# Four graph layers on one core: where the squares of adj are turned, and where the bias pieces of the attention are made

## The chip, the cores and the metric

The kernel runs on one core of one Trainium2 chip. The metric is the device time of one execution in microseconds, less is better. Before the change the median of 3 runs was 3029.25 us (3028.38 to 3029.67).

## The reference

x is 4096 x 256 and adj is 4096 x 4096, both float32. adj is symmetric in where it is nonzero, not in its values; some 0.8% of it is nonzero. Four layers follow one another, each wrapped in a residual sum and a LayerNorm over the 256 columns:

```
x = layernorm(x + attention(x, adj))       # layer 0: 4 heads of 64, scores + graph_bias * adj,
                                           #   -1e9 where adj == 0, softmax over the keys, @ Wout + bout
x = layernorm(x + gat(x, adj))             # layer 1: leaky_relu(src_i + dst_j), masked by adj > 0,
                                           #   softmax over j, @ (x @ W)
x = layernorm(x + gcn(x, adj))             # layer 2: D^-1/2 adj D^-1/2 @ x @ W.T + b
x = layernorm(x + relu(gcn(x, adj) @ W))   # layer 3
```

Layers 2 and 3 need adj with its rows on the free axis. The kernel makes a turned copy of adj, `adjT`, in the chip's memory beforehand and reads it back in those two layers.

## The kernel before, in words

One program per engine, written out by hand: what stands earlier in an engine's program runs earlier, and semaphores order the engines against one another. SP issues nearly all transfers, in program order; GpSimd (POOL) and ScalarE (ACT) issue a few.

**Layer 0, attention** (`layer0_attention`). 16 chunks of 256 query rows. A chunk goes over 4 heads, each in two halves: 8 sides, each of four beats r = 0 to 3, so that a place in the chunk is written (side, r). In a beat TensorE makes the scores of one piece of 128 x 1024 (L583; these belong to a head 12 beats ahead), turns exponentiated probabilities (L596), and at the end of the side multiplies them with the values (L609). VectorE reads each score piece out of PSUM, adding the bias and taking the maximum (`read_scores`, L869); ScalarE takes exponentials (L720) and copies turned pieces (L729). Three PSUM places of 128 x 1024 are used in turn, so TensorE can't write the third score piece of a side (r = 2) before VectorE has read the second (r = 1), nor turn its second piece of probabilities before VectorE has read r = 0.

The bias of the next chunk is 8 pieces of 128 x 1024 (i = 0 to 7). SP loads them at the 12th to the 19th beat. Six of them ("narrow") are masked by GpSimd in halves of 512 (L506), through three mask buffers, and VectorE finishes each with two operations of 128 x 512 (`make_bias`, L820). The other two (`WIDE`) are done by VectorE alone, in two operations of 128 x 1024 (`make_wide_bias`, L831 and L833). `MAKE_BIAS` says in which beat, after the score read, each piece is made; the first score piece that needs piece i is read at the beat i of side 5 on, (5, 0) for i = 0 up to (6, 3) for i = 7.

adjT is made here, in 256 blocks of 512 rows x 128 columns: SP loads a block (L397), VectorE turns its squares of 32 x 32 in one operation (`turn_block`, L889), SP stores it with four transfers of 64 KB (L408). Two buffers are used in turn, so VectorE waits before a block until the one two before has been stored. `BLOCKS_AT` gives the 17 beats of a chunk that turn a block each; the blocks last for 15 chunks and one more.

**Layer 1, graph attention** (the first half of `graph_layers`). 8 chunks c of 512 rows, each of 16 pairs. In a pair TensorE turns weights (L1462, `turn_pair`) and multiplies (L1479); ScalarE copies the turned weights out (L1604, `keep_pT`), then sums one item of 128 x 1024 of the next chunk's adj in place (L1586, `add_rows`), then takes one exponential (L1596); VectorE and GpSimd mask items (L1175), VectorE takes maxima (L1723) and logits (L1771). SP loads the next chunks' adj in four quarters of 1024 columns, 2 MB each, into `weight` (`load_adj`, L1255), two buffers of four quarters. Quarter n of chunk c + 2 is loaded once TensorE has turned 4(n + 1) pairs of chunk c. ScalarE comes to the items of quarter 3 of chunk c + 1 at pair 8 of chunk c. In VectorE's program `add_out` (L1788 and statistics) follows pair 4 and `ln.normalise` (L135) pair 7.

**Layers 2 and 3.** 8 chunks each. SP loads adjT (L1265), ScalarE and VectorE split it into a high and a low part (L1629, L1817), TensorE multiplies three times (L1532 to L1534).

## Time and profile before

| | before |
|---|---|
| median of 3 runs | 3029.25 us |
| profiled execution | 3032.35 us, of which its span is 3030.6 us |
| TensorE busy | 2951.2 us, 97% |
| VectorE busy | 2098.9 us, 69% |
| ScalarE busy | 1885.9 us, 62% |
| GpSimd busy | 769.0 us, 25% |
| attention, to about | 1615 us |
| layer 1, to about | 2205 us |
| layers 2 and 3, to the end | 3030.6 us |

The span is the time between the first and the last instruction of the profiled execution; 1.75 us of its own time lie around it. In rows of instructions the first number is the start, the second how long the group took; "idle before <- releaser" is how long the engine stood still and whose work ended that.

### The profile page before, as it was taken

To read this page: it belongs to the slowest core of one execution; us is meant where nothing else is said; L and a number is where in the kernel's file an instruction comes from. 1 tells how busy PE (TensorE), PEld (TensorE's weight loads), DVE (VectorE), ACT (ScalarE), POOL (GpSimd) and SP (SyncE) were. 2 spreads that over 40 slices of the span, in tenths; PEclk is the share of its full clock that TensorE was granted. 3 is DMA by queue.
4 is the path that set the end of the run, shared out by engine and by line. 5 is a ranking of instruction groups with operands and counts; after the bars stand their busy time and mean duration, and the time that the engine had idled before them with its cause. 6 is when DMAs were issued, how large, how long until landed. Compare 5 with 4: busy or idle time off the path is not lost.

```text
span 3030.6 us, 45417 instructions
## 1 busy us (share of the span) xinstructions
PE 2951.2 (97%) x16612; PEld 2181.2 (72%) x16612; DVE 2098.9 (69%) x3607; ACT 1885.9 (62%) x2705; POOL 769.0 (25%) x454
## 2 busy tenths in 40 slices
PE   8999999999999999999998899999999999999998
PEld 5777777777777777777776555555558888788886
DVE  6777777777777877787757977777535555565454
ACT  3677777777777777777775677777653333433332
POOL 2123321233212332133301455545501101000000
PEclk9999999999999999999999999999999999999999
DMA  6556676566755667566636333433179988989882
GB/s 186 158 170 198 198 211 180 170 197 196 216 162 180 199 188 227 156 184 205 189 101 257 124 125 130 148 126 125 32 183 214 214 200 201 221 209 217 199 200 58
DMA packets 412525, 534.42 MB, mean 176 GB/s; under 512 B 39440, under 2 KB 341776, under 8 KB 395920
## 3 DMA queue, kind: packets, MB, share of 16 engines
q1 hardware_dynamic: 387264, 445.00, 52.8%
q10 hardware_dynamic: 18144, 66.07, 7.1%
q0 software_dynamic: 6896, 20.45, 2.3%
q8 instruction: 133, 2.18, 0.3%
q14 instruction: 88, 0.72, 0.1%
HBM read 443.29 MB, written 88.08 MB: 175 GB/s over the span
## 4 chain that ended last, share of the span: by engine, by line
PE 80%; DVE 9%; issue 5%; DMA 3%; ACT 2%; POOL 1%; SPq 1%; DVEq 0%; POOLq 0%; ACTq 0%
PE at_o L609 12%; PE gl_four L1479 12%; PE at_turn L583 9%; PE at_turn L596 7%; PE gl_quad L1532 7%; PE gl_quad L1533 7%; PE gl_quad L1534 7%; PE at_score L583 4%; PE at_score L596 4%; PE gl_quad L1462 3%; DVE at_probs L869 2%; DVE at_bias L820 2%; PE gl_four L1505 2%; PE at_mixed L618 2%; DMA adjT<-at_probs 1%
## 5 line engine op out<-in xcount | busy, mean ns | idle before, releaser
L720 ACT ACTIVATE at_probs<-at_probs,at_minus_max 128x1024 f32<-128x1024 f32 x512 | 581.6, 1139 | 9.7 <-DVE at_minus_max L874 8.8
L869 DVE CUSTOM_DVE_ANT_0 at_probs<-at_turn,at_bias 128x1024 f32<-128x1024 f32 x336 | 407.3, 1212 | 170.2 <-PE at_turn L583 164.0
L506 POOL TENSOR_SCALAR at_masked<-at_bias 128x512 bf16<-128x512 f32 x180 | 378.2, 2116 | 537.7 <-DMA at_bias<-in_adj 405.4
L729 ACT ACTIVATE at_pT<-at_turn 128x1024 f32<-128x1024 f32 x342 | 346.0, 1024 | 235.4 <-PE at_turn L596 235.3
L609 PE MATMUL at_o<-at_pT,at_values 128*64 128x256 f32 x4096 | 470.3, 382 | 0.0
L1479 PE MATMUL gl_four<-gl_early,gl_first_wh 128*128 128x512 f32 x1024 | 462.3, 594 | 4.6 <-ACT gl_early L1604 4.6
L1629 ACT ACTIVATE gl_split<-gl_units 128x1024 fp32r<-128x1024 f32 x256 | 263.8, 1055 | 278.6 <-PE gl_quad L1534 278.6
L1532 PE MATMUL gl_quad<-gl_split,gl_rows_hi 128*128 128x512 f32 x1024 | 402.3, 393 | 5.0 <-DVE gl_split L1817 5.0
L609 PEld LDWEIGHTS at_o<-at_pT,at_values 128*64 128x64 f32 x4096 | 282.4, 137 | 172.8 <-issue 43.2
L583 PE MATMUL at_turn<-at_kT,at_q 128*128 128x512 f32 x1344 | 396.0, 416 | 10.3 <-DVE at_maxima L869 10.3
L1533 PE MATMUL gl_quad<-gl_split,gl_rows_hi 128*128 128x512 f32 x1024 | 398.5, 389 | 0.0
L1534 PE MATMUL gl_quad<-gl_split,gl_rows_lo 128*128 128x512 f32 x1024 | 398.5, 389 | 0.0
L1817 DVE TENSOR_TENSOR gl_split<-gl_units,gl_split 128x1024 fp32r<-128x1024 f32 x256 | 306.2, 1222 | 116.2 <-ACT gl_split L1629 115.7
L596 PE MATMUL at_turn<-all_ident,at_probs 128*128 128x128 f32 x2736 | 349.3, 273 | 5.3 <-DVE at_maxima L869 2.9
L596 PEld LDWEIGHTS at_turn<-all_ident,at_probs 128*128 128x128 f32 x2736 | 313.8, 140 | 44.7 <-DVE at_maxima L869 9.0
L1479 PEld LDWEIGHTS gl_four<-gl_early,gl_first_wh 128*128 128x128 f32 x1024 | 185.3, 191 | 190.3 <-issue 185.0
L1175 POOL TENSOR_SCALAR gl_first_weights<-gl_first_weights 128x1024 f32<-128x1024 f32 x57 | 237.4, 4165 | 268.1 <-ACT gl_first_weights L1586 268.1
L583 PEld LDWEIGHTS at_turn<-at_kT,at_q 128*128 128x128 f32 x1344 | 227.8, 189 | 73.9 <-issue 30.6
L869 DVE CUSTOM_DVE_ANT_0 at_probs<-at_score,at_bias 128x1024 f32<-128x1024 f32 x176 | 213.4, 1212 | 93.3 <-PE at_score L583 90.4
L729 ACT ACTIVATE at_pT<-at_score 128x1024 f32<-128x1024 f32 x170 | 174.1, 1024 | 114.0 <-PE at_score L596 113.9
L889 DVE STREAM_TRANSPOSE at_probs<-at_probs 128x512 f32<-128x512 f32 x256 | 181.2, 708 | 84.1 <-DMA adjT<-at_probs 83.5
L1604 ACT ACTIVATE gl_early<-gl_quad 128x1024 f32<-128x1024 f32 x128 | 131.0, 1023 | 157.2 <-PE gl_quad L1462 157.2
(135 smaller groups left out, 3871.0 us busy)
## 6 DMA issues: line engine op xcount, KB each, us to landing
gl_units<-adjT SPq DMA_DIRECT2D x512, 256.0 KB, 7.8
at_bias<-in_adj SPq DMA_DIRECT2D x128, 512.0 KB, 6.5
at_probs<-in_adj SPq DMA_DIRECT2D x256, 256.0 KB, 3.7
adjT<-at_probs SPq DMA_DIRECT2D x1024, 64.0 KB, 3.0
gl_first_weights<-in_adj SPq DMA_DIRECT2D x32, 2048.0 KB, 8.2
at_values<-v_heads ACTq DMA_DIRECT2D x126, 512.0 KB, 4.4
gl_early<-x SPq DMA_DIRECT2D x160, 128.0 KB, 2.6
x<-gl_early POOLq DMA_DIRECT2D x64, 128.0 KB, 2.8
```

Source lines behind the costliest of these rows:

```text
L506: pool.tensor_scalar(masked[:, g % MASKS, :], part, 0.0, MASKED / SCALE, ALU.is_equal, ALU.mult)\
L583: last = pe.matmul(place[:, at], q[:, q_place(h), part, t * P:(t + 1) * P], kT[:, h, col:col + BANK], start=part == 0, stop=part == 1)
L596: last = pe.transpose(place[:, a * CN + t * P:a * CN + (t + 1) * P], ring[:, place_in_ring(s, m // BEATS), t, m % BEATS * P:(m % BEATS + 1 ...
L609: last = pe.matmul(o_bank[side * HD:(side + 1) * HD, 0:CN], values[:, q, a, :], pT[:, slot, a % GROUP * CN:(a % GROUP + 1) * CN], start=q ...
L720: act.activation(part, part, ACT.Exp, bias=minus_max[:, k, t:t + 1], scale=1.0, accum_out=sums[:, k, t, pp:pp + 1]).then_inc(prob_ready, 1)
L729: act.activation(pT[:, j % PT_SLOTS, :], place[:], ACT.Copy).then_inc(pT_ready, 1)
L869: dve.tensor_tensor_reduce(out=ring[:, place_in_ring(u, pp), t, :], in0=place[:], in1=bias[:, t, at], scale=SCALE, scalar=LOWEST, op0=ALU. ...
L1479: last = pe.matmul(out_bank1[c % 2][half], wh[:, m * D + half * P:m * D + (half + 1) * P], pT[:, g % PT_RING, part * CN:(part + 1) * CN], ...
L1532: pe.matmul(out_bank3[r % 2][half], rows_hi[:, at], block_hi, start=first, stop=False)
L1533: pe.matmul(out_bank3[r % 2][half], rows_hi[:, at], block_lo, start=False, stop=False)
L1534: last = pe.matmul(out_bank3[r % 2][half], rows_lo[:, at], block_hi, start=False, stop=final)
L1817: dve.tensor_tensor(split3[:, slot, 1, :], tiles[:, n, part:part + 2 * CN], split3[:, slot, 0, :].bitcast(F32), ALU.subtract).then_inc(lo3 ...
```

## The change

Eight of the 32 blocks of 128 columns of each of six sets of 512 rows (sets 2 to 7, columns 3072 to 4095: 48 of 256 blocks) are no longer turned in the attention. They are turned in layer 1, the second layer, out of quarter 3 of the adj chunk that lies in `weight` for that layer anyway, so they aren't loaded for it. VectorE turns two blocks each after pairs 3, 5, 6 and 7 of chunks 1 to 6, through two buffers; SP stores each with four transfers, in its program between the loads of quarters 0 and 1 of chunk c + 2; ScalarE doesn't go on at pair 8, which overwrites that quarter in place, before all eight have been turned. The attention has 208 blocks left, and three of the 17 beats of a chunk, (4, 2), (5, 0) and (6, 3), turn none.

The bias pieces are made at other beats: 1 and 2 together at (4, 3), 3 at (5, 1), 4 and 5 together at (5, 3), 6 at (6, 1), 7 at (6, 2), and none at (5, 2) and (6, 0). The two wide pieces are 2 and 5 in place of 3 and 6.

```diff
-    MAKE_BIAS = {(4, 1): 0, (4, 3): 1, (5, 1): 2, (5, 2): 3, (5, 3): 4, (6, 0): 5, (6, 1): 6, (6, 2): 7}
+    MAKE_BIAS = {(4, 1): (0,), (4, 3): (1, 2), (5, 1): (3,), (5, 3): (4, 5), (6, 1): (6,), (6, 2): (7,)}
...
-    ROW_BLOCKS = N // P
-    BLOCKS = NT // BLOCK_TILES * ROW_BLOCKS
+    LATE_BLOCKS = 8
+    SET_BLOCKS = N // P
+    ROW_BLOCKS = SET_BLOCKS - LATE_BLOCKS
+    WHOLE_SETS = 2
+    BLOCKS = WHOLE_SETS * LATE_BLOCKS + NT // BLOCK_TILES * ROW_BLOCKS
...
-    BLOCKS_AT = {(0, 0): 1, (0, 2): 1, (1, 0): 1, (1, 2): 1, (2, 1): 1, (2, 2): 1, (2, 3): 1, (3, 0): 1, (3, 1): 1, (3, 2): 1, (4, 0): 1, (4, 2): 1, (5, 0): 1, (6, 3): 1, (7, 0): 1, (7, 1): 1, (7, 2): 1}
+    BLOCKS_AT = {(0, 0): 1, (0, 2): 1, (1, 0): 1, (1, 2): 1, (2, 1): 1, (2, 2): 1, (2, 3): 1, (3, 0): 1, (3, 1): 1, (3, 2): 1, (4, 0): 1, (7, 0): 1, (7, 1): 1, (7, 2): 1}
...
-    WIDE = (3, 6)
+    WIDE = (2, 5)
...
-                        if (side, r) in MAKE_BIAS and not last:
-                            i = MAKE_BIAS[side, r]
+                        for i in () if last else MAKE_BIAS.get((side, r), ()):
...
+    LATE_AT = {3: (0, 1), 5: (2, 3), 6: (4, 5), 7: (6, 7)}
...
+        turned_squares = early[:, 4096:4096 + 2 * CN].rearrange("p (b k t i) -> p b k t i", b=2, k=BLOCK_KEYS, t=CT)
...
+            def store_late(c, k):
+
+                b = LATE_BLOCKS * (c + 1 - WHOLE_SETS) + k
+                n = N // P - LATE_BLOCKS + k
+                sync.wait_ge(late_turned, b + 1)
...
+                for g in range(SQUARES):
+                    rows = slice(g * CT * SQUARE, (g + 1) * CT * SQUARE)
+                    sync.dma_start(to[:, (c + 1) * (N // CN) + n * P // CN, at:at + BLOCK_KEYS, rows],
+                                   turned_squares[g * SQUARE:(g + 1) * SQUARE, b % 2, :, :, :].rearrange("j k t i -> j k (t i)"))\
+                        .then_inc(late_stored[b % 2], 16)
...
+                    if n == 0 and c + 1 >= WHOLE_SETS:
+                        for k in range(LATE_BLOCKS):
+                            store_late(c, k)
+            for stored_late in late_stored:
+                sync.wait_ge(stored_late, 16 * SQUARES * LATE_BLOCKS * (CHUNKS - WHOLE_SETS) // 2)
...
+                if c >= WHOLE_SETS and n == QUARTERS - 1 and t == 0:
+                    act.wait_ge(late_turned, LATE_BLOCKS * (c + 1 - WHOLE_SETS))
...
+            def turn_late(c, k):
+
+                b = LATE_BLOCKS * (c + 1 - WHOLE_SETS) + k
+                n = QUARTERS - 1
+                dve.wait_ge(adj_loaded[(c + 1) % 2 * QUARTERS + n], 16 * ((c + 1) // 2 + 1))
+                wait(dve, late_stored[b % 2], 16 * SQUARES * (b // 2))
+                block = weight[:, (c + 1) % 2, n, :, k * P:(k + 1) * P]
+                dve.transpose(turned_squares[:, b % 2, :, :, :], block.rearrange("p t (k i) -> p k t i", i=SQUARE))\
+                   .then_inc(late_turned, 1)
...
                     logits(e - 3)
+                    if WHOLE_SETS <= c + 1 < CHUNKS:
+                        for k in LATE_AT.get(pair, ()):
+                            turn_late(c, k)
                     if pair == 4 and c:
                         add_out(c - 1)
```

## Rows read from the trace of the kernel before

**Rows 1.** The page: busy time of each engine

```profile
PE 2951.2 (97%) x16612; PEld 2181.2 (72%) x16612; DVE 2098.9 (69%) x3607; ACT 1885.9 (62%) x2705; POOL 769.0 (25%) x454
```

**Rows 2.** Windows, a chunk each of attention and layer 1: length, PE, PEld, DVE, ACT, POOL, PEclk

```profile
480.30:575.70 95.40, 94.42 (x672) 73.14 (x671) 73.84 (x141) 71.76 (x106) 26.70 (x14) 1.00 0.63 192
...
1882.00:1953.00 71.00, 70.03 (x265) 38.09 (x264) 54.28 (x83) 51.50 (x81) 37.09 (x15) 1.00 0.36 133
```

**Rows 3.** TensorE in order of time, attention: its idle times, four of them

```profile
173.11 1.19 PE L583 MATMUL at_score<-at_kT,at_q 128*128 128x512 f32 x4 [0.98 <-DVE at_maxima L869]
...
553.60 1.19 PE L583 MATMUL at_turn<-at_kT,at_q 128*128 128x512 f32 x4 [0.98 <-DVE at_maxima L869]
...
817.85 1.20 PE L583 MATMUL at_score<-at_kT,at_q 128*128 128x512 f32 x4 [2.49 <-DVE at_maxima L869]
...
1508.99 1.19 PE L583 MATMUL at_turn<-at_kT,at_q 128*128 128x512 f32 x4 [0.98 <-DVE at_maxima L869]
```

**Rows 4.** VectorE in order of time, sides 5 and 6 of the same chunk

```profile
538.14 1.23 DVE L869 CUSTOM_DVE_ANT_0 at_probs<-at_score,at_bias 128x1024 f32<-128x1024 f32 x1 [1.90 <-PE at_score L583]
...
544.04 1.05 DVE L831 TENSOR_SCALAR at_xs<-at_bias 128x1024 bf16<-128x1024 f32 x1
545.13 1.51 DVE L833 SCALAR_TENSOR_TENSOR at_bias<-at_bias,at_gain,at_xs 128x1024 f32<-128x1024 f32 x1
546.67 1.23 DVE L869 CUSTOM_DVE_ANT_0 at_probs<-at_turn,at_bias 128x1024 f32<-128x1024 f32 x1
...
547.82 1.41 DVE L820 SCALAR_TENSOR_TENSOR at_bias<-at_bias,at_gain,at_masked 128x512 f32<-128x512 f32 x2
549.36 1.23 DVE L869 CUSTOM_DVE_ANT_0 at_probs<-at_turn,at_bias 128x1024 f32<-128x1024 f32 x1
...
550.51 1.76 DVE L820 SCALAR_TENSOR_TENSOR at_bias<-at_bias,at_gain,at_masked 128x512 f32<-128x512 f32 x2
```

**Rows 5.** TensorE in the same sides: last scores of side 5, two turnings of side 6

```profile
543.06 1.17 PE L583 MATMUL at_turn<-at_kT,at_q 128*128 128x512 f32 x4
...
550.65 1.09 PE L596 MATMUL at_turn<-all_ident,at_probs 128*128 128x128 f32 x8
551.58 1.04 PE L596 MATMUL at_score<-all_ident,at_probs 128*128 128x128 f32 x8
```

**Rows 6.** The lines L831 and L833: duration ns min/median/max

```profile
L831 DVE TENSOR_SCALAR at_xs<-at_bias x30: 704/877/1049, 163.6 to 1508.9; 128x1024 bf16<-128x1024 f32 x30
...
L833 DVE SCALAR_TENSOR_TENSOR at_bias<-at_bias,at_gain,at_xs x30: 1283/1394/1509, 164.6 to 1509.6; 128x1024 f32<-128x1024 f32 x30
```

**Rows 7.** The page: the turning of the blocks

```profile
L889 DVE STREAM_TRANSPOSE at_probs<-at_probs 128x512 f32<-128x512 f32 x256 | 181.2, 708 | 84.1 <-DMA adjT<-at_probs 83.5
```

**Rows 8.** GpSimd in order of time, the masks of the same chunk

```profile
542.18 4.69 POOL L506 TENSOR_SCALAR at_masked<-at_bias 128x512 bf16<-128x512 f32 x2 [2.26 <-DVE at_bias L820]
```

**Rows 9.** ScalarE in order of time, the same chunk, pairs 8 and 9

```profile
2004.80 1.05 ACT L1586 ACTIVATE gl_first_weights<-gl_first_weights 128x1024 f32<-128x1024 f32 x1
...
2008.19 1.02 ACT L1604 ACTIVATE gl_early<-gl_quad 128x1024 f32<-128x1024 f32 x1 [1.12 <-PE gl_quad L1462]
```

**Rows 10.** SP in order of time, the same chunk, from 1975 to 1990 us

```profile
1982.21 0.38 SPq L1255 DMA_DIRECT2D gl_first_weights<-in_adj  x1
```

**Rows 11.** Transfers by line, issue to landing: L408 (block stores), L1255 (quarters), L1292

```profile
L408 SPq DMA_DIRECT2D adjT<-at_probs x1024: 302/456/3051, 101.6 to 1532.8; - x171
DMA to landing us min/median/max: 1.6/3.0/7.9
...
DMA to landing us min/median/max: 7.9/8.1/8.4
...
DMA to landing us min/median/max: 7.7/7.7/7.7
```

**Rows 12.** VectorE in order of time, layer 1, pairs 5 and 7 of a chunk

```profile
1988.67 0.69 DVE L1175 TENSOR_SCALAR gl_first_weights<-gl_first_weights 128x1024 f32<-128x1024 f32 x1 [0.55 <-ACT gl_first_weights L1586]
...
1997.29 0.69 DVE L1175 TENSOR_SCALAR gl_first_weights<-gl_first_weights 128x1024 f32<-128x1024 f32 x1 [2.15 <-ACT gl_first_weights L1586]
```

More of the change, by code:

```diff
@@ L355, in block_at @@
         def block_at(b):
-            return b // ROW_BLOCKS, b % ROW_BLOCKS
+            if b < WHOLE_SETS * SET_BLOCKS:
+                return b // SET_BLOCKS, b % SET_BLOCKS
+            b -= WHOLE_SETS * SET_BLOCKS
+            return WHOLE_SETS + b // ROW_BLOCKS, b % ROW_BLOCKS
         def place_of(g):
@@ L1009, in graph_layers @@
     XS_RING = 4
+    BLOCK_KEYS = P // SQUARE
+    LATE_BLOCKS = 8
+    WHOLE_SETS = 2
+    LATE_AT = {3: (0, 1), 5: (2, 3), 6: (4, 5), 7: (6, 7)}
     HALF_BIG = QUARTERS * CT * QC
@@ L1125, in graph_layers @@
         multiplied3, projected = sp.sem("multiplied3"), sp.sem("projected")
+        late_turned, late_stored = sp.sem("late_turned"), [sp.sem(f"late_stored{k}") for k in range(2)]
         outT_ready = [sp.sem(f"outT_ready{i}") for i in range(DH)]
@@ L1256, in load_adj @@
                     .then_inc(adj_loaded[c % 2 * QUARTERS + n], 16)
+            def store_late(c, k):
+                b = LATE_BLOCKS * (c + 1 - WHOLE_SETS) + k
+                n = N // P - LATE_BLOCKS + k
+                sync.wait_ge(late_turned, b + 1)
+                to = adjT.rearrange("j (s k r) -> j s k r", k=CN // SQUARE, r=CN)
+                at = n * BLOCK_KEYS % (CN // SQUARE)
+                for g in range(SQUARES):
[3 more added lines that the diff above has]
+                        .then_inc(late_stored[b % 2], 16)
             def load_set(r, n):
```

## The prediction

> **What bounds the kernel now.** I read the page first. TensorE is busy 97% of the span, VectorE 69% [rows 1]: only what TensorE waits for can be won, at most some 80 us over all stages. Then stretches of one chunk: TensorE works 94.42 of 95.40 us in a chunk of the attention and 70.03 of 71.00 in one of layer 1, so it misses 0.98 and 0.97 us in each, at a granted clock of 1.00 [rows 2]: there is no clock to win back. Then TensorE in order of time. In the attention there is one idle time of 0.98 us in each chunk, always at the same place: 14 of them from 173.11 to 1508.99, about 95.4 us apart (a fifteenth, near 937, would be among the few records that a trace loses; the pattern of VectorE's rows is there too). An odd one of 2.49 us stands at 817.85, a smaller one later [rows 3]. The wait is for a score read of VectorE.
>
> VectorE's rows show why. In sides 5 and 6 it goes without a pause from 538.14 on: score read, bias piece, score read, bias piece. The wide piece at (5, 2) takes 2.60 us (544.04 to 546.64), and the read of (5, 3) starts only at 546.67, though its scores were made by 544.23. From there the backlog is carried on: (6, 0) is read at 549.36, a slow narrow piece of 1.76 us ends at 552.27, and the read of (6, 1), 1.15 us, begins only then [rows 4, 5]. TensorE, done with its turnings at 552.62, can write the next scores only then: 553.60 [rows 3, 5]. The 0.97 us in layer 1 are no score read's, and the change takes nothing from that stage.
>
> **Attention, the bias pieces.** I replay sides 4 to 6 with the durations of this chunk, with TensorE as it was.
> - (4, 3) gets piece 2 after piece 1. VectorE stood idle 1.90 us before the read at 538.14. A wide piece takes 1.99 to 2.56 us (0.704 + 1.283 to 1.049 + 1.509, [rows 6]), and the block that went from (4, 2) gives back some 0.2: the read of (5, 0) comes up to 0.5 us later. But (5, 0) no longer turns a block (0.71 us, [rows 7]), so (5, 1) is read when it was. TensorE's next need of (5, 0) is over a microsecond after its end. Cost nothing; the cover is that idle time, and without it the cost would be the 0.5.
> - (5, 1) makes one narrow piece as before. (5, 2) makes none, so its read ends at 544.04 and (5, 3) is read as soon as its scores are there, at about 544.4 in place of 546.67: 2.3 us earlier.
> - (5, 3) makes a narrow piece (1.41) and a wide one. If the wide takes 2.60, as at (5, 2) [rows 4], VectorE comes to (6, 0) at 544.4 + 1.15 + 1.41 + 2.65 = 549.6, against 549.36; if it takes 2.0, at 549.0. I take the slow value: GpSimd's masks run then, as they ran at 542.18 to 546.87 beside the slow one [rows 8].
> - (6, 0) makes none: its read ends at 550.76 (before at 550.51), and TensorE's second turning, which began at 550.65 right behind it [rows 5], comes 0.1 to 0.25 us late. (6, 1) is then read at 550.9, ends at 552.1, and TensorE, ready at 552.7 to 552.9, no longer waits. (6, 1) and (6, 2) make one narrow piece each with 1.5 us of air.
>
> So 0.98 us go and 0.1 to 0.25 come: 0.8 us gained in each of 15 chunks, **12 us**; the ends are 0.98 x 15 = 14.7 and, should the shift to (6, 0) be 0.5, 7. GpSimd's order becomes 0, 1, 3, 4, 6, 7 through the same three buffers. Its halves, about 2.1 us each, are released by VectorE's pieces; the tightest is the last half of piece 7, released near 552.8, done near 555.0, wanted near 555.8. Piece 2's load is issued three beats after piece 0's was made possible, over 10 us ahead. Nothing.
>
> **Attention, the blocks.** 48 x 0.708 = 34 us of VectorE and a share of its 84.1 us of waiting for stores leave [rows 7], with 48 loads and 192 stores on SP's queue. TensorE is the bound, so this is worth only what it gives to the waits above, already counted. The two odd waits stand beside slow stores in side 3 and (4, 0), where the blocks stay: I count 0; at the most some 4 us would go.
>
> **Layer 1, what is added.** In each of six chunks VectorE gets 8 x 0.708 = 5.7 us, SP 32 issues. VectorE is busy 54.28 of 71 us [rows 2], so the work fits; the question is the order. TensorE is three stages away: VectorE turns, ScalarE waits for all eight at pair 8 before its sum (2004.80), and TensorE needs ScalarE's exponential of pair 11 at pair 12. ScalarE idles 1.12 us a pair there [rows 9], so it makes up 3 x 1.12 = 3.4 us before TensorE notices. Blocks all turned by 2004.80 cost nothing; up to 2008.2 still nothing.
> The chain, in the chunk whose quarter 0 is issued at 1982.21, as pair 3 has been turned [rows 10]. Quarter 3 was issued at the end of the chunk before, over three pairs of 4.3 us earlier, and lands in 8.1 [rows 11]; at pair 3 it is there. Blocks 0 and 1 follow, 1.4 us. They push `add_out` back, which hid 0.55 us of idle, so pair 5 begins at 1989.55 instead of 1988.67 and ends, 3.3 us on, at 1992.85 [rows 12]. Blocks 2 and 3 need the stores of 0 and 1. These stand on SP's queue behind the 2 MB load issued at 1982.21, which lands at 1990.3. Small transfers behind such a load land with it: the 256 KB of L1292 needed 7.7 us [rows 11]. So they land at 1991.5 to 1994, and VectorE waits 0 to 1 us. Blocks 2 and 3 are turned by 1994.3. Pair 6's work takes 3.15 us and ends at 1997.45 instead of 1995.14; it had 2.15 us of idle behind it [rows 12]. Four stores take 4 x 0.48 us to issue and 3.0 to land, 4.5 us after the turning, and 6.4 for the second block of a pair [rows 11]: blocks 4 and 5 go at 1998.1 and 2000.0. Pair 7's 3.3 us end at 2004.0, block 6 goes then, block 7 at 2005.2, done at 2005.9. ScalarE waits 1.1 us, with the first wait added 2.1: under 3.4. **Cost taken: 0.** The lower end is 0 (nothing there gives a gain). For the upper one I take landings of 5 us, between the median and the longest: the last block is done at 2009.9, ScalarE waits 5.1, TensorE 1.7, times six = 10 us.
> The load of quarter 1 of chunk c + 2 now stands behind the eight stores and is issued some 8 us later; ScalarE wants it 30 us after that. `ln.normalise` comes 6 us later, GpSimd's store and mask behind it under 1 us. Layers 2 and 3 read the same bytes.
>
> **Sum.** 12 - 0 = 12 us. The profiled execution's own 3032.35 becomes 3020.3; it lay 3.1 us above the median, so the median goes from 3029.25 to **3017.2**.
>
> **Rivals.**
> 1. *The wait moves instead of going* (chance 0.20, with partial costs in layer 1). The read of (6, 0) ends so late that its own wait takes over: VectorE's two narrow operations at (5, 3) take the slow 1.76 and the wide piece 2.6, and TensorE waits 0.6 of the 0.98. For it: the margin before 550.65 is 0.14 us. Against it: 2.3 us are won before. Gain 6 or less: 3023 to 3029. Layer 1 with landings of 5 us gives 3027.
> 2. *ScalarE held at pair 8* (0.09), the one on the other side. Stores behind the 2 MB load, then through two buffers in pairs: with landings of 6 us, which stores in the attention reach under load (longest 7.9, [rows 11]), the eighth block is done at 2011.9, ScalarE waits 7.1, TensorE 3.7, times six = 22 us: 3039. It decides from a ScalarE wait of 3.4 us on, and is slower than before from 5.4. Against it: between two quarter loads the queue is empty.
> 3. *VectorE locked out by GpSimd at (5, 3)* (0.03). A wide operation that begins within a mask would stand until that mask of 2.1 us ends: (6, 0) would be read near 551, TensorE would wait 1.7 in place of 0.98, +11 us: 3040. The trace speaks against it: beside masks from 542.18 to 546.87 the two wide operations took 1.05 and 1.51, 0.35 and 0.23 over the shortest ones, not 2 [rows 4, 6, 8]. The Trainium skill, SBUF — State Buffer, section "SBUF: two separate sides", has the rule: the port pair of VectorE and GpSimd is an exclusive lock and the later of the two fully blocks. By it the sum would be this rival's; by the row it is mine.
>
> The rest, 0.68, is the forecast, 3012 to 3022. What one measurement here can tell from no change is about 0.2%, 6 us: 3023.2 to 3035.3. Faster 0.68, same 0.20, slower 0.12. The range goes from 3011 (both odd waits gone as well) to 3029 (most of rival 1).
>
> **What would show it.** Right: no idle time of 0.98 us in front of L583 once a chunk; L596 in side 6 waiting under 0.3 us; chunks of the attention 94.6 us long; chunks 1 to 6 of layer 1 still 71.2 us; ScalarE waiting for VectorE 0 to 3 us at pair 8, VectorE some 1 us for stores. Wrong: a wait of TensorE before L1462 at pair 12, chunks of layer 1 over 72 us, or a wait of the old size at another read of side 5 or 6.

## The result, and the profile after the change

**3009.96 us**, the median of four runs of the changed kernel (three took 3009.59 to 3010.27 us; in the fourth TensorE was granted only 0.654 of its clock and the time was 4296 us, so the profile below is that of a repeated execution), against 3029.46 us for the kernel before beside them: ratio 0.9932, interval 0.9913 to 0.9952. That is 19.5 us faster where 12 was forecast (3017.2), and 1 us below the lower end of the range. The direction was right. The size was not, and most of what follows is about that.

The page of the changed kernel, a repeated execution of 3010.49 us with a span of 3008.8 us:

```profile
PE 2943.9 (98%) x16612; PEld 2180.7 (72%) x16612; DVE 2094.7 (70%) x3607; ACT 1886.0 (63%) x2705; POOL 772.9 (26%) x454
...
L895 DVE STREAM_TRANSPOSE at_probs<-at_probs 128x512 f32<-128x512 f32 x208 | 147.2, 708 | 64.1 <-DMA adjT<-at_probs 63.5 <-issue 0.3
```

No engine's work changed by more than 8 us ([rows 1]). The span is 21.8 us shorter, and TensorE's busy time 7.3: a third of the gain lies in time that had been listed as work. Two windows, a chunk of the attention and one of layer 1, in the columns of [rows 2]:

```profile
493.60:587.50 93.90, 93.90 (x674) 73.07 (x670) 71.11 (x135) 71.58 (x106) 27.64 (x14) 1.00 0.60 177
1943.00:2014.20 71.20, 70.23 (x264) 38.10 (x264) 59.49 (x90) 51.62 (x82) 35.10 (x16) 1.00 0.50 163
```

The idle time of 0.98 us is gone from the attention's chunk, and the chunk is 1.5 us shorter, not 1. Layer 1's chunk keeps its length, with 5.2 us more of VectorE in it. TensorE in order of time, in side 6 (lines moved down by 6: L589 is L583 of before, L602 is L596), and behind it the same place of the kernel before:

```profile
541.44 1.21 PE L589 MATMUL at_turn<-at_kT,at_q 128*128 128x512 f32 x4
542.49 1.03 PE L602 MATMUL at_score<-all_ident,at_probs 128*128 128x128 f32 x8
543.28 1.17 PE L589 MATMUL at_turn<-at_kT,at_q 128*128 128x512 f32 x4
544.29 1.03 PE L602 MATMUL at_turn<-all_ident,at_probs 128*128 128x128 f32 x8
545.16 1.04 PE L602 MATMUL at_score<-all_ident,at_probs 128*128 128x128 f32 x8
545.95 1.17 PE L589 MATMUL at_turn<-at_kT,at_q 128*128 128x512 f32 x4
```

```profile
547.76 1.20 PE L583 MATMUL at_turn<-at_kT,at_q 128*128 128x512 f32 x4
548.80 1.03 PE L596 MATMUL at_score<-all_ident,at_probs 128*128 128x128 f32 x8
549.59 1.17 PE L583 MATMUL at_turn<-at_kT,at_q 128*128 128x512 f32 x4
```

Read the starts, counted from the side's first scores (541.44 and 547.76). The second turning begins 2.85 us in (before: 2.89, [rows 5]), the turning after it 3.72 in (before 3.82), the third scores 4.51 in (before 553.60, so 5.84, [rows 3]). The side is 1.33 us shorter.

VectorE in the same stretch:

```profile
538.05 1.22 DVE L875 CUSTOM_DVE_ANT_0 at_probs<-at_turn,at_bias 128x1024 f32<-128x1024 f32 x1 [0.48 <-PE at_turn L589]
...
539.21 1.41 DVE L826 SCALAR_TENSOR_TENSOR at_bias<-at_bias,at_gain,at_masked 128x512 f32<-128x512 f32 x2
540.53 1.10 DVE L837 TENSOR_SCALAR at_xs<-at_bias 128x1024 bf16<-128x1024 f32 x1
541.67 1.28 DVE L839 SCALAR_TENSOR_TENSOR at_bias<-at_bias,at_gain,at_xs 128x1024 f32<-128x1024 f32 x1
542.87 1.22 DVE L875 CUSTOM_DVE_ANT_0 at_probs<-at_turn,at_bias 128x1024 f32<-128x1024 f32 x1
...
544.60 1.22 DVE L875 CUSTOM_DVE_ANT_0 at_probs<-at_turn,at_bias 128x1024 f32<-128x1024 f32 x1 [0.50 <-PE at_turn L589]
```

(5, 3) is read at 538.05, which is 2.3 us earlier against the side's start than at [rows 4]; then its narrow piece, its wide one, and the read of (6, 0) at 542.87. The read of (6, 1) now waits 0.50 us for TensorE, where TensorE used to wait for it.

**Where the time went, by stage.** Layer 1 takes one small reduction over its maxima for each chunk (L1781, L1750 before: `gl_max_dst<-gl_max_part`); the first and the last of these eight serve as marks near its start and its end. Worked out from their starts in the two profiles: up to the first 1668.4 became 1644.6 (-23.8 us), from first to last 498.3 became 497.8 (-0.5), behind it 863.9 became 866.4 (+2.5). The sum is the 21.8 us of the spans; the medians differ by 19.5 here and by 19.7 when both kernels were run again. Within the attention, the sides from one value product (L615, L609 before) to the next, worked out from the time lines of 15 chunks:

```
us                       side 4 mean   side 5 median   side 6 median
before                      12.26          10.99           13.21
after                       12.12          11.01           11.88
after, a later profile      12.19          11.00           11.87
pieces alone                12.23          11.27           11.87
squares alone               12.13          10.99           13.21
new beats, wide 3, 6        12.29          11.55           12.37
old beats, wide 2, 5        12.21          10.99           13.28
blocks moved                12.21          11.01           11.87
all other sides of both: 10.99 (1), 11.85 to 11.87 (0, 2, 7), 12.3 (3)
```

Side 6 gives 1.31 to 1.35 us in 14 of the 15 chunks and 1.7 in one, 20.4 us. Side 4's mean gives 0.14 in this pair of profiles, 2 us. That is 22 of the 23.8, but the 2 us of side 4 are not shown to be the change's: in the six profiles whose attention is that of the changed kernel its mean is 12.12 to 12.29 us, and the 12.26 of before lies among them. Those six profiles come to the first reduction after 1643.0 to 1647.3 us, so some 4 us of the 23.8 are no more than what repeated executions differ by.

### The profile page after: what moved, and what is told of

It is laid out like the page before. It is cut to its first block, busy times and chain, and to the rows that moved or that the text cites. A ratio compares the mean times of both kernels' runs of the same rounds, so it can differ in the third digit from the quotient of the medians.

```text
span 4294.3 us, 45374 instructions
## 1 busy us (share of the span) xinstructions
PE 4269.7 (99%) x16612; PEld 2573.3 (60%) x16612; DVE 2102.1 (49%) x3607; ACT 1914.1 (45%) x2705; POOL 744.2 (17%) x454
## 4 chain that ended last, share of the span: by engine, by line
PE 98%; issue 1%; DVE 0%; ACT 0%; DMA 0%; POOLq 0%; POOL 0%; DVEq 0%; ACTq 0%
PE at_o L615 16%; PE gl_four L1508 16%; PE at_turn L589 10%; PE at_turn L602 10%; PE gl_quad L1563 7%; PE gl_quad L1561 7%; PE gl_quad L1562 7%; PE at_score L589 5%; PE at_score L602 5%; PE gl_quad L1491 4%; PE at_mixed L624 2%; PE gl_four L1534 2%; PE at_turn L541 1%; PE at_mixed L569 1%; PE at_o L550 1%
## 5 line engine op out<-in xcount | busy, mean ns | idle before, releaser
L1508 PE MATMUL gl_four<-gl_early,gl_first_wh 128*128 128x512 f32 x1024 | 691.9, 839 | 0.0
L615 PE MATMUL at_o<-at_pT,at_values 128*64 128x256 f32 x4096 | 687.2, 512 | 0.0
L589 PE MATMUL at_turn<-at_kT,at_q 128*128 128x512 f32 x1344 | 532.6, 533 | 0.3
L615 PEld LDWEIGHTS at_o<-at_pT,at_values 128*64 128x64 f32 x4096 | 310.5, 156 | 360.4 <-issue 154.0
L1561 PE MATMUL gl_quad<-gl_split,gl_rows_hi 128*128 128x512 f32 x1024 | 524.2, 512 | 0.0
L1563 PE MATMUL gl_quad<-gl_split,gl_rows_lo 128*128 128x512 f32 x1024 | 519.3, 507 | 0.0
L1562 PE MATMUL gl_quad<-gl_split,gl_rows_hi 128*128 128x512 f32 x1024 | 518.8, 507 | 0.0
L602 PE MATMUL at_turn<-all_ident,at_probs 128*128 128x128 f32 x2736 | 500.1, 347 | 1.4 <-ACT at_pT L735 1.1
L602 PEld LDWEIGHTS at_turn<-all_ident,at_probs 128*128 128x128 f32 x2736 | 405.4, 163 | 106.8 <-issue 28.9
L1508 PEld LDWEIGHTS gl_four<-gl_early,gl_first_wh 128*128 128x128 f32 x1024 | 213.8, 215 | 338.8 <-issue 336.6
L589 PEld LDWEIGHTS at_turn<-at_kT,at_q 128*128 128x128 f32 x1344 | 268.7, 213 | 126.1 <-issue 67.9
L1635 ACT ACTIVATE gl_early<-gl_quad 128x1024 f32<-128x1024 f32 x128 | 130.9, 1023 | 433.4 <-PE gl_quad L1491 433.4
L1562 PEld LDWEIGHTS gl_quad<-gl_split,gl_rows_hi 128*128 128x128 f32 x1024 | 212.7, 208 | 122.0 <-issue 41.2
```

The costliest lines, as they stand in the source:

```text
L589: last = pe.matmul(place[:, at], q[:, q_place(h), part, t * P:(t + 1) * P], kT[:, h, col:col + BANK], start=part == 0, stop=part == 1)
L602: last = pe.transpose(place[:, a * CN + t * P:a * CN + (t + 1) * P], ring[:, place_in_ring(s, m // BEATS), t, m % BEATS * P:(m % BEATS + 1 ...
L615: last = pe.matmul(o_bank[side * HD:(side + 1) * HD, 0:CN], values[:, q, a, :], pT[:, slot, a % GROUP * CN:(a % GROUP + 1) * CN], start=q ...
L1508: last = pe.matmul(out_bank1[c % 2][half], wh[:, m * D + half * P:m * D + (half + 1) * P], pT[:, g % PT_RING, part * CN:(part + 1) * CN], ...
L1561: pe.matmul(out_bank3[r % 2][half], rows_hi[:, at], block_hi, start=first, stop=False)
L1562: pe.matmul(out_bank3[r % 2][half], rows_hi[:, at], block_lo, start=False, stop=False)
```

## The experiments

Each kernel stands against runs of the kernel before that were made beside it. Their median was 3030.82 us for the first four experiments (up to the one with nearly no late squares), 3030.94 for new beats, old beats, the late squares a pair later and the spread exponentials, 3032.45 for the moved blocks and the crowded squares, 3031.53 for the second repeat and the two edits together. The intervals of these ratios are 0.0008 to 0.0016 wide to each side, 2.5 to 5 us.

**The same kernel again.** No edit.

> The changed kernel once more, for a profile at full clock. All theories expect about 3010 us, 19.5 under the kernel before. What they disagree on is where the trace shows it. Theory A (the wait of 0.98 us a chunk, and nothing else): TensorE shows no idle time before the score matmuls in the fifteen chunks, 14.7 us, and the odd waits are as before, some 5 us stay unexplained. Theory B (the odd waits of 2.49 and 1.33 us went too, since fewer blocks compete with the bias loads): those two are missing, 14.7 + 3.8 = 18.5 us. Theory C (layer 1 got shorter): the seven spans of layer 1 are under 71.2 us a chunk.

3011.08 us, ratio 0.9932 (0.992 to 0.9945): the same ratio to the fourth place. Later, again with no edit:

> The changed kernel once more, beside the other on the same chip: 19 to 20 us under the kernel before.

3011.51, ratio 0.9938 (0.9925 to 0.9952). Its stages are 1645.3, 497.9 and 866.5 us, so the 2.5 us that the end is longer are there again. Of the three theories none is right as it stands: A has the place and not the size, B's odd waits are dealt with below, and C finds the chunks of layer 1 at 71.2 us as before.

**The bias pieces alone,** in the kernel before:

```diff
-    MAKE_BIAS = {(4, 1): 0, (4, 3): 1, (5, 1): 2, (5, 2): 3, (5, 3): 4, (6, 0): 5, (6, 1): 6, (6, 2): 7}
+    MAKE_BIAS = {(4, 1): (0,), (4, 3): (1, 2), (5, 1): (3,), (5, 3): (4, 5), (6, 1): (6,), (6, 2): (7,)}
...
-    WIDE = (3, 6)
+    WIDE = (2, 5)
...
-                        if (side, r) in MAKE_BIAS and not last:
-                            i = MAKE_BIAS[side, r]
+                        for i in () if last else MAKE_BIAS.get((side, r), ()):
```

> Only the other beats for the bias pieces and VectorE's pieces 2 and 5; all 256 blocks are turned in the attention in the 17 beats of before. Theory A: the block at (5, 0) now stands behind a later read, (5, 1) is read about 0.5 us later and TensorE waits 0.3 to 0.5 us at the third score piece of side 5; 0.5 to 0.7 us a chunk are won: 7 to 11 us. Theory B: the same, 7 to 11 us, and the odd waits stay. If the whole gain were the bias order's, 19.5 us.

**3014.95 us**, 15.9 less than before (ratio 0.9943, 0.9931 to 0.9956), where 7 to 11 was expected: the wait had been priced too low here too. **The squares alone**, the changed kernel with the two old tables:

```diff
-    MAKE_BIAS = {(4, 1): (0,), (4, 3): (1, 2), (5, 1): (3,), (5, 3): (4, 5), (6, 1): (6,), (6, 2): (7,)}
+    MAKE_BIAS = {(4, 1): (0,), (4, 3): (1,), (5, 1): (2,), (5, 2): (3,), (5, 3): (4,), (6, 0): (5,), (6, 1): (6,), (6, 2): (7,)}
...
-    WIDE = (2, 5)
+    WIDE = (3, 6)
```

> Only the blocks: 48 are turned in layer 1 and the three beats are free, while the bias pieces are made as before and VectorE does 3 and 6. Theory A: the read of (5, 1) was bound by its scores, so the backlog of (5, 2) to (6, 1) stays and with it the 0.98 us; 0 us won. Theory B: 3 to 5 us won, by the odd waits. A theory that the blocks themselves were what cost the 0.98 us would expect 15 or more.

**3029.82 us**, 1.0 less, and 1 within the interval (0.9987 to 1.0005). Its TensorE has the old wait at the old place:

```profile
551.64 1.20 PE L589 MATMUL at_turn<-at_kT,at_q 128*128 128x512 f32 x4 [0.98 <-DVE at_maxima L875]
```

So the pieces make the gain. But 15.9 and 1.0 are 3 short of the 19.7 that both bring. The intervals alone would not show so small a difference; the trace does: with the pieces alone side 5 is 11.27 us long and not 11.01, 0.26 x 15 = 3.9 us. VectorE there, with the pieces alone:

```profile
528.40 0.71 DVE L889 STREAM_TRANSPOSE at_probs<-at_probs 128x512 f32<-128x512 f32 x1
...
531.18 1.40 DVE L820 SCALAR_TENSOR_TENSOR at_bias<-at_bias,at_gain,at_masked 128x512 f32<-128x512 f32 x2
532.50 1.10 DVE L831 TENSOR_SCALAR at_xs<-at_bias 128x1024 bf16<-128x1024 f32 x1
533.63 1.28 DVE L833 SCALAR_TENSOR_TENSOR at_bias<-at_bias,at_gain,at_xs 128x1024 f32<-128x1024 f32 x1
534.83 1.22 DVE L869 CUSTOM_DVE_ANT_0 at_probs<-at_score,at_bias 128x1024 f32<-128x1024 f32 x1
...
535.98 0.71 DVE L889 STREAM_TRANSPOSE at_probs<-at_probs 128x512 f32<-128x512 f32 x1
```

and TensorE:

```profile
533.10 1.19 PE L583 MATMUL at_score<-at_kT,at_q 128*128 128x512 f32 x4
...
536.11 1.09 PE L596 MATMUL at_score<-all_ident,at_probs 128*128 128x128 f32 x8
```

The block at (4, 2) stands ahead of the double beat, and the read of (5, 0) begins 1.73 us behind the side's first scores (534.83 - 533.10; in the changed kernel 1.37, 531.80 - 530.43). The second turning, 3.01 us in, comes 0.17 late for it (2.84 in the changed kernel); the block at (5, 0) then holds up (5, 1) as well. No row lists this as idle time of the matmuls.

**Nearly no late squares.** 46 of the 48 late turnings are left out, so those parts of adjT are not turned; the loads, the stores and all else stay:

```diff
-                sync.wait_ge(late_turned, b + 1)
+                sync.wait_ge(late_turned, min(b + 1, 2))
...
-                    act.wait_ge(late_turned, LATE_BLOCKS * (c + 1 - WHOLE_SETS))
+                    act.wait_ge(late_turned, 2)
...
-                    if WHOLE_SETS <= c + 1 < CHUNKS:
+                    if c == 1 and pair == 3:
```

> The changed kernel, but VectorE turns only the first two of the 48 late blocks, and SP stores these two in the place of all; ScalarE waits for nothing more. It leaves out 46 turnings in layer 1 (33 us of VectorE), with the waits that go with them. If the late turnings are hidden, as predicted, the time is that of the changed kernel within 1 us; if ScalarE's wait at pair 8 reaches TensorE, it is faster by up to 10 us.

3010.99 us, against 3011.08 with all of them: what the turnings cost in layer 1 is nothing that can be measured.

**The blocks moved within the attention.** The kernel with the pieces alone, all 256 blocks in the attention, but none at (4, 2) and (5, 0):

```diff
-    BLOCKS_AT = {(0, 0): 1, (0, 2): 1, (1, 0): 1, (1, 2): 1, (2, 1): 1, (2, 2): 1, (2, 3): 1, (3, 0): 1, (3, 1): 1, (3, 2): 1, (4, 0): 1, (4, 2): 1, (5, 0): 1, (6, 3): 1, (7, 0): 1, (7, 1): 1, (7, 2): 1}
+    BLOCKS_AT = {(0, 0): 1, (0, 1): 1, (0, 2): 1, (1, 0): 1, (1, 1): 1, (1, 2): 1, (2, 1): 1, (2, 2): 1, (2, 3): 1, (3, 0): 1, (3, 1): 1, (3, 2): 1, (4, 0): 1, (6, 3): 1, (7, 0): 1, (7, 1): 1, (7, 2): 1}
```

> The bias pieces as in the changed kernel, all 256 blocks turned in the attention, in 17 beats, but (4, 2) and (5, 0) turn none and (0, 1) and (1, 1) do, where VectorE idles. Theory A (the squares had only to leave the beats around the bias pieces): side 5 is back from 11.27 to 11.0 us, and the time is that of the changed kernel within 3 us, near 3011. Theory L (they had to leave the attention, for the transfers or for VectorE's waits for stores): it stays near 3015, or is slower, VectorE waiting for the stores at (0, 1) and (1, 1) and TensorE for it.

3009.13 us, ratio 0.9927 (0.9915 to 0.994): as good as the change, with no late square at all. VectorE waits longer for stores than before (84.1 us, [rows 7]), and it costs nothing:

```profile
L889 DVE STREAM_TRANSPOSE at_probs<-at_probs 128x512 f32<-128x512 f32 x256 | 181.3, 708 | 103.4 <-DMA adjT<-at_probs 102.6 <-issue 0.3
```

What the squares gave was the freedom of two beats, not less work. The two blocks were moved together; which of the two beats matters more was not tried.

**Beats and wide pieces apart.** The changed kernel with only one of its two tables old:

```diff
-    WIDE = (2, 5)
+    WIDE = (3, 6)
```

> The changed kernel with the new beats for the bias pieces, but VectorE alone does 3 and 6 as before, GpSimd the others. Theory A (what counts is that (5, 2) and (6, 0) make nothing, and so VectorE comes to (6, 0) and (6, 1) in time): 3 at (5, 1) takes about 1 us more and (5, 3) about 1 us less; within 4 us of the changed kernel. Theory W (the choice of pieces 2 and 5 counts too, since pairs of narrow pieces need four masked halves at once and there are three buffers): VectorE waits for GpSimd at (4, 3) and (5, 3), and 0.3 us or more a chunk are lost, 5 us or more over the changed kernel.

3027.2 us (ratio 0.999, 0.9981 to 0.9999), 3.7 less than before: 16 of the 20 us are lost again. VectorE:

```profile
532.78 2.42 DVE L826 SCALAR_TENSOR_TENSOR at_bias<-at_bias,at_gain,at_masked 128x512 f32<-128x512 f32 x3
536.00 1.09 DVE L826 SCALAR_TENSOR_TENSOR at_bias<-at_bias,at_gain,at_masked 128x512 f32<-128x512 f32 x1 [0.80 <-POOL at_masked L512]
...
547.50 1.08 DVE L826 SCALAR_TENSOR_TENSOR at_bias<-at_bias,at_gain,at_masked 128x512 f32<-128x512 f32 x1 [0.80 <-POOL at_masked L512]
```

A double beat of two narrow pieces wants four masked halves at once, and three buffers hold three. The fourth is masked only after VectorE has freed one; VectorE stands 0.80 us in each double beat. Sides 5 and 6 are 0.54 and 0.49 us longer, 1.03 x 15 = 15.5 us of the 16. The other table alone:

```diff
-    MAKE_BIAS = {(4, 1): (0,), (4, 3): (1, 2), (5, 1): (3,), (5, 3): (4, 5), (6, 1): (6,), (6, 2): (7,)}
+    MAKE_BIAS = {(4, 1): (0,), (4, 3): (1,), (5, 1): (2,), (5, 2): (3,), (5, 3): (4,), (6, 0): (5,), (6, 1): (6,), (6, 2): (7,)}
```

> The changed kernel with the beats of before for the bias pieces, but VectorE alone does 2 and 5. Theory A: the wide pieces stand at (5, 1) and (6, 0); the read of (5, 3) comes at the same time as before, that of (6, 1) about 0.5 us later, so that side 6 takes some 13.7 us and the time is 3030 to 3038. If the choice of the pieces were the cause of the gain, it would be near 3011.

3031.76 us (ratio 1.0006, 0.9997 to 1.0014), side 6 at 13.28. Counted from the squares alone (1.0 us less than before), the new beats by themselves give 2.7 us, the new wide pieces by themselves lose 1.8, and both together give 18.7. With three mask buffers, one piece of each double beat must be the kind that needs no mask.

**The late squares a pair later,** to find where ScalarE's slack ends:

```diff
-    LATE_AT = {3: (0, 1), 5: (2, 3), 6: (4, 5), 7: (6, 7)}
+    LATE_AT = {5: (0, 1), 6: (2, 3), 7: (4, 5), 8: (6, 7)}
```

> The changed kernel with the late blocks turned after pairs 5, 6, 7 and 8 in place of 3, 5, 6 and 7. ScalarE's wait at pair 8 becomes about 5.2 us. If it can make up 3 x 1.12 = 3.4 us before TensorE needs its exponential, as predicted, TensorE loses 1.8 us in each of six chunks and the time is 11 us over the changed kernel (8 to 16). If its slack is larger than taken, no change; if TensorE feels ScalarE's wait at once, over 25 us.

3012.68 us, 1 to 2 more than the changed kernel, where 11 was expected. ScalarE waits at pair 8 in all six chunks: 2.79, 2.83, 3.43, 3.45 and 3.29 us, and 5.73 in the last. Two of them, in order of time:

```profile
1985.41 1.06 ACT L1617 ACTIVATE gl_first_weights<-gl_first_weights 128x1024 f32<-128x1024 f32 x1 [3.45 <-DVE gl_early L1813]
...
2130.09 1.06 ACT L1617 ACTIVATE gl_first_weights<-gl_first_weights 128x1024 f32<-128x1024 f32 x1 [5.73 <-DVE gl_early L1813]
```

and TensorE behind the longest of them:

```profile
2130.88 1.04 PE L1491 MATMUL gl_quad<-all_ident,gl_first_weights 128*128 128x128 f32 x8
2133.33 3.70 PE L1508 MATMUL gl_four<-gl_early,gl_first_wh 128*128 128x512 f32 x8 [1.42 <-ACT gl_early L1635]
...
2137.74 3.60 PE L1508 MATMUL gl_four<-gl_early,gl_first_wh 128*128 128x512 f32 x8
2141.66 1.09 PE L1491 MATMUL gl_quad<-all_ident,gl_first_weights 128*128 128x128 f32 x8 [0.32 <-ACT gl_first_weights L1627]
```

The chunks with 3.43 and 3.45 us are 71.20 us long, so these waits are hidden whole. Of the 5.73 us TensorE loses 2.2, counted from start to start: 2.45 us from 2130.88 to 2133.33 where 0.87 is usual, 0.1 in the group behind it, and 3.92 from 2137.74 to 2141.66 where 3.43 is usual. (The idle time listed is 1.42 and 0.32.) So TensorE notices from 5.73 - 2.2 = 3.5 us on. There are two waits in it. The last is at pair 12, for the exponential of pair 11, as forecast. The first and larger one is for ScalarE's copy of pair 9's turned weights (L1635), the next thing that ScalarE owes; the forecast had not seen it, and it alone would begin at 5.73 - 1.58 = 4.15 us. The waits at pair 8 are shorter than I had expected; the stores land sooner (below).

**All late squares in two pairs:**

```diff
-    LATE_AT = {3: (0, 1), 5: (2, 3), 6: (4, 5), 7: (6, 7)}
+    LATE_AT = {7: (0, 1, 2, 3), 8: (4, 5, 6, 7)}
```

> The changed kernel with four late blocks after pair 7 and four after pair 8, through the same two buffers. Each block but the first two waits for the store of the one two before, so the eighth is done some 10 to 16 us after ScalarE comes to pair 8. If ScalarE's slack is 3.4 us, TensorE loses the rest in each of six chunks, 40 to 75 us in all, and the chunks of layer 1 are longer by ScalarE's wait minus 3.4. If TensorE lost the whole wait, the chunks would be longer by the wait itself.

**3073.74 us**, ratio 1.014 (1.0125 to 1.0156). Rival 2 in full: ScalarE waits 76.8 us in six, 12.3 to 13.8 each, and TensorE 8.0 to 9.5 each, for the copy of pair 9 and not at pair 12. TensorE:

```profile
1863.39 6.27 PE L1508 MATMUL gl_four<-gl_early,gl_first_wh 128*128 128x512 f32 x8 [8.02 <-ACT gl_early L1635]
1869.49 1.04 PE L1491 MATMUL gl_quad<-all_ident,gl_first_weights 128*128 128x128 f32 x8
1870.37 3.60 PE L1508 MATMUL gl_four<-gl_early,gl_first_wh 128*128 128x512 f32 x8
```

and the windows of this stretch and of the next:

```profile
1863.40:1870.00 6.60, 6.60 (x13) 3.01 (x14) 5.67 (x6) 5.19 (x9) 4.60 (x1) 0.61 0.82 309
1870.00:1876.00 6.00, 6.00 (x24) 3.21 (x23) 4.13 (x8) 4.25 (x7) 3.29 (x1) 1.00 0.72 261
```

The stage is 564.2 us long in place of 497.8, 11.1 a chunk. The idle time is 8.0 to 9.5 of it; most of the rest is that the eight matmuls behind it take 5.1 to 6.4 us in place of 3.60: in the row shown at a granted clock of 0.61, which then is 1.00 again.

**The other 0.97 us.** The wait that layer 1 has in most chunks (six times in all, [rows 2]) is for ScalarE's exponentials of the next chunk, two in each of the last two pairs. Spread over three pairs:

```diff
-                    elif pair >= PAIRS - 2 and c + 1 < CHUNKS:
-                        for t in range(2):
-                            exponential(ITEMS * (c + 1) + 2 * (pair - PAIRS + 2) + t)
+                    elif c + 1 < CHUNKS:
+                        for t in {13: (0,), 14: (1, 2), 15: (3,)}.get(pair, ()):
+                            exponential(ITEMS * (c + 1) + t)
```

> The changed kernel, and of the four exponentials that ScalarE takes ahead for the next chunk of layer 1 the first goes to pair 13, two stay at pair 14 and one at pair 15 (they were two and two). It tests how a stall is to be read: the idle column has 0.97 us at the start of each chunk, 7 x 0.97 = 6.8 us; the spacing of ScalarE's copies there is 5.50 us where it is 4.31 elsewhere, 7 x 1.19 = 8.3 us. If that wait is all there is, the time falls by one of the two, to about 3003.

**3002.1 us**, 9.0 less than the changed kernel, ratio 0.9905 (0.9892 to 0.9919). ScalarE at the chunk's end, changed kernel:

```profile
2009.90 1.02 ACT L1635 ACTIVATE gl_early<-gl_quad 128x1024 f32<-128x1024 f32 x1
...
2015.40 1.02 ACT L1635 ACTIVATE gl_early<-gl_quad 128x1024 f32<-128x1024 f32 x1 [1.18 <-PE gl_quad L1491]
```

and with the exponentials spread:

```profile
2003.64 1.02 ACT L1635 ACTIVATE gl_early<-gl_quad 128x1024 f32<-128x1024 f32 x1
...
2008.01 1.02 ACT L1635 ACTIVATE gl_early<-gl_quad 128x1024 f32<-128x1024 f32 x1 [1.18 <-PE gl_quad L1491]
```

The two copies stand 5.50 us apart in the one and 4.37 in the other, and TensorE's starts say the same: from 2009.70 to 2014.27 in the changed kernel, 4.57 us, where the same two groups are 3.44 apart in the spread one. That is 1.13 us in each of six places, 6.8 us (the expectation's seven places and its 1.19 were both too many). The idle column lists 0.97 each, 5.8. By the marks of its reductions layer 1 is 491.0 us long in place of 497.8, 6.8 less, and its chunks 70.07 in place of 71.20: start to start is right again and the idle column short again. The medians' 9.0 could not have decided between the two, with intervals of some 4 us to each side; another 2 us of it lie behind layer 1 and have another cause (the next section, layers 2 and 3).

**Moved blocks and spread exponentials:** the kernel of the moved blocks with the edit just shown.

> The bias pieces of the changed kernel, all 256 blocks in the attention in the beats of blocks_moved, and the exponentials of layer 1 spread as in exp_spread. If the gains add up and the late turnings in layer 1 were worth nothing, it is 8 to 9 us under the changed kernel, near 3001. If the late turnings gave something that blocks_moved hid, it is 3 us or more over exp_spread.

3002.54 us, ratio 0.9911 (0.9898 to 0.9925). With the one before it this is the fastest kernel of the study, 9 us ahead of the change and 29 ahead of before; the interval doesn't tell the two apart. Its layer 1 is 6.8 us shorter than that of the moved blocks (491.4 in place of 498.2).

## Why the prediction was wrong in size, point by point

- **The wait that goes: 0.98 us a chunk, times 15.** This is the step that failed: the term 0.98 x 15 = 14.7 us of the sum was priced too low, and it measured 20.4. The wait was found, placed and explained rightly, and all of it went; but it was worth 1.33 us. (The fifteenth, which I took for lost from the trace, is there, at 937.00 with 0.98.) I priced it by the idle time in front of L583, and that is counted from the modelled end of the group before. That group, at 551.58, is listed with 1.04 us and would have ended at 552.62; yet where nothing is waited for, the next one begins 0.79 us after its start (545.16 to 545.95 after the change). So 553.60 - 551.58 - 0.79 = 1.23 us were lost there, and 0.1 more before it, in the turning that began 3.82 and not 3.72 us in. 1.33 x 15 = 20.0 where I had 14.7. The Trainium skill, Perfetto Trace Analysis, section "Identifying the Most-Contended Engine", warns that the busy share of TensorE's pipelined matmuls is no good measure of how close a kernel is to what the engine can do. The trace agrees: TensorE's busy time fell by 7.3 us with the same 16612 matmuls. That the idle time is listed short for the same reason is what these runs add: 0.98 listed and 1.33 won here, 0.97 listed and 1.13 won by the spread exponentials. The rows of before had it: a spacing of 2.02 us where the same pair of groups elsewhere takes 0.79.
- **0.1 to 0.25 us come back at (6, 0).** They did not. The read begins 1.43 us into the side (542.87 - 541.44) in place of 1.60. I had taken 2.60 us for the wide piece; at (5, 3) it took 1.10 + 1.28, 2.34 from its start to the next read. The term was -2.7 us, and measured 0: the second step of the sum that was mis-sized.
- **(5, 3) is read 2.3 us earlier, (6, 1) no longer holds TensorE.** Both as forecast; it now is VectorE that waits 0.50 us.
- **(4, 3) costs nothing.** Right for the change as a whole: the read of (5, 0) begins 1.37 us into the side, as before (538.14 [rows 4] with the side's first scores at 536.77). Its condition was the 1.90 us of idle time. The reason was only half the right one: I named the block of (5, 0), and the pieces alone show that the block of (4, 2), which I had put at "some 0.2", eats the same cover: 3.9 us with both in place.
- **The blocks are worth only what they give to the waits, the odd waits 0, at most 4.** The squares alone are 1.0 us, within the measurement. The two odd waits of before, 2.49 us at 817.85 and 1.33 at 1102.9, are gone, but that says nothing about the blocks: in the twelve other full-clock profiles no wait of TensorE for a score read beyond the first 95 us is over 1.2 us, and three of the twelve turn all 256 blocks in the attention. They look like one execution's own, so nothing here shows that the change wins them.
- **GpSimd's order: nothing.** Right, with a condition that I had not seen: pieces 2 and 5 being wide is what keeps three buffers enough, and with pieces 3 and 6 wide the same beats lose 16 us.
- **Layer 1: cost 0.** Right. Its chunks are 71.20 us, VectorE waits 9.8 us for stores in 12 waits, ScalarE 1.0 us in 3, the longest 0.53; two squares in place of 48 measure the same. From the waits of layer 1:

```profile
DVE gl_early L1813 <- DMA adjT<-gl_early: 9.8, 12, 1.8
...
ACT gl_first_weights L1617 <- DVE gl_early L1813: 1.0, 3, 0.5
```

- **The rivals.** 1, the wait moves: no wait for a score read is left in side 6. 2, ScalarE held at pair 8: it exists, but it takes more than a pair's delay to bring it about. Its threshold is 3.5 us where I had 3.4, by the path through pair 12 that I had named; the other path, the copy of pair 9, was missing and is the one that waits longest. 3, VectorE locked out by GpSimd: GpSimd ran four masks from 535.85 to 544.73, and the wide operations beside them took 1.10 and 1.28 us, at most 0.4 over their shortest; nothing stood for a mask's 2 us. The trace speaks against the rule, as it did before.

- **Layers 2 and 3 read the same bytes: nothing.** Their bytes are the same, yet 2.5 us are lost behind layer 1, a term that I had put at nothing in one sentence. Where layer 1 passes into layer 2, TensorE waits twice for ScalarE, 22 us apart. Before (the first two rows) and after:

```profile
2192.04 5.25 PE L1479 MATMUL gl_four<-gl_early,gl_first_wh 128*128 128x512 f32 x8 [2.49 <-ACT gl_early L1604]
...
2213.84 3.70 PE L1479 MATMUL gl_four<-gl_early,gl_first_wh 128*128 128x512 f32 x8 [1.88 <-ACT gl_early L1604]
```

```profile
2167.77 3.70 PE L1508 MATMUL gl_four<-gl_early,gl_first_wh 128*128 128x512 f32 x8 [2.44 <-ACT gl_early L1635]
...
2189.68 5.40 PE L1508 MATMUL gl_four<-gl_early,gl_first_wh 128*128 128x512 f32 x8 [3.53 <-ACT gl_early L1635]
```

  One of the two groups of eight matmuls is slow in each: before it is the first (granted clock 0.69 from 2192.0 to 2197.2), after it is the second:

```profile
2189.70:2195.00 5.30, 5.30 (x9) 2.23 (x10) 1.86 (x5) 5.30 (x11) 0.00 (x0) 0.68 0.41 124
```

  The second wait ends with ScalarE's rows of x, and their load goes out 36.2 us behind the last reduction of layer 1 in both kernels (2202.87 - 2166.7 and 2178.60 - 2142.4). So the second group starts at the same time in both, some 47.2 us behind that reduction. A slow first group only shortens the wait that follows: before, 5.25 us of matmuls and 1.88 of waiting; after, 3.70 and 3.53. A slow second group has nothing behind it to hide in, and costs its 1.7 us. The rest of the 2.5, 0.7 us, lies further on, and no row here explains it. The thirteen full-clock profiles sort themselves by this alone: where the second group is slow the part behind the last reduction is 865.2 to 868.4 us long, where it is not, 862.8 to 864.5.

**The sum.** The forecast was 14.7 - 2.7 = 12. Measured are 20.4 for the wait, 0 for the shift to (6, 0), 0 for layer 1 and 2.5 lost behind it, 18. The medians differ by 19.5 to 20.0 and the spans of the two single profiles by 21.8; the 2 to 4 us between are of the size by which profiles of one kernel differ, and no row accounts for them.

**Left open.** Why the clock falls behind the first of the two waits in some kernels and behind the second in others. The first group is the slow one in all four profiles with every block in the attention and in those of the squares a pair later and the crowded squares; the second in the changed kernel's own two and in four more with late squares or their stores; neither in that of the spread exponentials. The turnings themselves are not the cause: with 46 of the 48 left out, the second is slow all the same (3.38 us of waiting, 5.40 for the eight). The spread exponentials have neither slow, and most of the 2 us that they gain behind layer 1 is that. No run moved the load of x ahead of the eight loads of adjT (L1289) in front of it, which would shorten the second wait.

## What to carry to other kernels

Price a stall of TensorE by the distance between the starts of two groups, against the same two groups at a place where nothing waits, and not by the idle time listed in front of the second. Before laying a loss to a longer wait, see whether the engine only came to it earlier and leaves it at the same time. When work that comes one piece a beat is doubled up, ask at once what each piece needs of the shared buffers, and what else stands in the beats just ahead of the double one: here the two tables were worth 2.7 us and less than nothing apart, and 18.7 together. Work that must leave a crowded beat may be as well off a few beats further on as in another layer.

## What the runs showed of the hardware that I had not expected

- A wait of TensorE can cost more than its own length. Behind waits of 8.0 to 9.5 us the next eight matmuls took 6.4 to 5.1 us in place of 3.60, at granted clocks of 0.57 to 0.72, between the lower of the two levels (1.2 GHz of 2.4, 0.5) and the full one. The shorter waits had the slower matmuls: 8.00 us were followed by 6.39, 9.50 by 5.13.
- The length of a wait doesn't decide by itself whether the clock falls. At the step from layer 1 to layer 2 the eight matmuls took 5.24 to 5.40 us (granted 0.67 to 0.70 in the seven of these groups whose window was read) behind waits of 2.43 to 3.64 us, and 3.70 behind others of 1.41 to 3.21. The overlap is wide: 2.43 us were followed by a slow group with the pieces alone and by a fast one with the squares alone.
- The late stores land in 1.8 us (median) where I had taken the 3.0 of the attention [rows 11], the longest in 8.5. The long ones stand behind a 2 MB load: eight stores issued 0.6 to 4.4 us behind the load of 1958.00 landed in 5.5 to 8.0 us. The loads suffer too: 9.1 us (median) in place of 8.1; those of 1958.00 and 1984.04, beside stores, took 9.5 and 10.0, the next two, with no stores beside them, 8.3 and 8.1. The lines L1278 (stores) and L1266 (load), issue to landing:

```profile
DMA to landing us min/median/max: 1.6/1.8/8.5
...
DMA to landing us min/median/max: 7.9/9.1/10.6
```
